# A decoder layer over 16 batches: q and k projected two batches ahead, layer-norm closings moved into the next batch's score stage

## The reference, cut to what matters

```python
# x (16, 256, 128), context (16, 64, 128); all float32
xn  = layernorm(x) * gamma
q, k, v = xn @ w_q, *split(xn @ w_kv)        # 16 heads of 64
q, k = l2norm(q) * q_scale, l2norm(k) * k_scale
s   = 8 * q @ k.T  - slope[head] * distance, with 2 null keys, causal
x   = layernorm(x + softmax(s) @ v @ w_out)
x   = layernorm(x + cross_attention(x, context))   # 16 heads of 8
x   = layernorm(x + ((x @ W1[g].T + b1[g]) @ W2[g].T + b2[g]))  # group g of 2 batches
```

## Time and profile before

| | us |
|---|---|
| median of 3 runs (1008.38 to 1009.17) | 1009.04 |
| the profiled execution's own time | 1014.34 |
| its span, first to last instruction | 1012.2 |
| TensorE busy, of the span | 849.9 (84%) |
| VectorE busy | 802.7 (79%) |
| ScalarE busy | 660.7 (65%) |
| GpSimd busy | 425.7 (42%) |

### The profile page before, as it was taken

The page is one execution under the profiler, slowest core; times in us unless marked ns, Lnnn a source line. Parts: engine busy times, 40 slices in busy tenths (PEclk is TensorE's granted clock), DMA queues, the critical chain, the costliest instruction groups (busy, mean ns, idle before and its releaser), DMA issues.

```text
span 1012.2 us, 18717 instructions
## 1 busy us (share of the span) xinstructions
PE 849.9 (84%) x6181; PEld 663.4 (66%) x6181; DVE 802.7 (79%) x2564; ACT 660.7 (65%) x1938; POOL 425.7 (42%) x356
## 2 busy tenths in 40 slices
PE   6898888888888898888889889888888888888774
PEld 5667666765766676576767657666765766676552
DVE  6665779788888978898897888788787988888545
ACT  4475767757685766767676675767667576766532
POOL 0244162543616253361635346173534617253431
PEclk9799999999999999999999999999999999999795
DMA  6000000000100000000100001000100001000000
GB/s 189 6 1 6 6 27 7 6 12 6 28 12 6 6 13 26 6 6 12 27 6 7 11 6 28 11 6 7 27 11 7 6 12 27 1 6 6 6 1 10
DMA packets 26414, 15.56 MB, mean 15 GB/s; under 512 B 4304, under 2 KB 25552, under 8 KB 26320
## 3 DMA queue, kind: packets, MB, share of 16 engines
q1 hardware_dynamic: 26320, 14.38, 5.0%
HBM read 12.27 MB, written 2.10 MB: 14 GB/s over the span
## 4 chain that ended last, share of the span: by engine, by line
PE 45%; DVE 25%; ACT 18%; issue 6%; POOL 4%; DMA 2%; DVEq 0%; ACTq 0%; POOLq 0%
PE psY L600 12%; ACT pr L1319 9%; PE psS L566 6%; PE psT L586 5%; PE psS L636 4%; ACT sq L1291 3%; POOL pr L1519 3%; PE psJ L441 3%; PE psS L548 3%; PE psJ L443 2%; PE psJ L442 2%; DVE xp L1061 2%; DVE xmax L1059 2%; DVE ssq L957 2%; ACT xpT L1367 2%
## 5 line engine op out<-in xcount | busy, mean ns | idle before, releaser
L1519 POOL TENSOR_TENSOR pr<-pr,rden 128x512 f32<-128x512 f32 x192 | 192.9, 1040 | 379.2 <-ACT pr L1319 195.8
L600 PE MATMUL psY<-val,pT 128*128 128x128 f32 x1536 | 206.5, 281 | 31.3 <-ACT pT L1334 23.7
L1319 ACT ACTIVATE pr<-pr,nmin 128x256 f32<-128x256 f32 (+1 forms) x512 | 225.3, 443 | 10.8 <-DVE nmin L1004 10.2
L600 PEld LDWEIGHTS psY<-val,pT 128*128 128x128 f32 x1536 | 186.6, 193 | 41.8 <-issue 22.2
L1004 DVE CUSTOM_DVE_ANT_0 pr<-psS,alibi,nullmin 128x256 f32<-128x256 f32 (+1 forms) x512 | 183.7, 414 | 26.4 <-PE psS L566 24.4
L1510 POOL TENSOR_TENSOR qk<-qk,rn 128x1024 f32<-128x1024 f32 x64 | 121.1, 1913 | 88.8 <-DVE x L870 50.2
L586 PE MATMUL psT<-ident,pr 128*128 128x128 f32 x768 | 116.9, 279 | 20.2 <-POOL pr L1519 20.2
L566 PE MATMUL psS<-kT,qT 64*128 64x256 f32 (+1 forms) x1024 | 111.7, 346 | 19.3 <-DVE nmin L1004 12.9
L586 PEld LDWEIGHTS psT<-ident,pr 128*128 128x128 f32 x768 | 88.9, 143 | 39.9 <-POOL pr L1519 32.7
L566 PEld LDWEIGHTS psS<-kT,qT 64*128 64x128 f32 x1024 | 78.2, 189 | 48.5 <-DVE nmin L1004 19.4
L1319 ACT ACTIVATION_READ_ACCUMULATOR pr<-pr,nmin 128x1 f32 x512 | 96.6, 189 | 0.0
(11 more groups left out here) (138 smaller groups left out, 1663.5 us busy)
## 6 DMA issues: line engine op xcount, KB each, us to landing
w1s<-w1b SPq DMA_DIRECT2D x8, 258.0 KB, 2.9
xin<-x SPq DMA_DIRECT2D x16, 128.0 KB, 2.1
xres<-x SPq DMA_DIRECT2D x16, 128.0 KB, 2.1
w2s<-w2T SPq DMA_DIRECT2D x8, 256.0 KB, 3.2
out<-x SPq DMA_DIRECT2D x16, 128.0 KB, 1.8
pr<-w_q SPq DMA_DIRECT2D x1, 512.0 KB, 3.8
pr<-w_kv SPq DMA_DIRECT2D x1, 512.0 KB, 5.0
pr<-wvT SPq DMA_DIRECT2D x1, 512.0 KB, 4.5
```

Of the source, the lines that this page charges most:

```text
L600: mm = pe.matmul(psY[t], pT[c % 4][:, P * j:P * (j + 1)], val[:, kt, P * h:P * (h + 1)], start=(blk == 0), stop=False)
L1319: act.activation(pr[t][:, h, :], pr[t][:, h, :], ACT.Exp, bias=nmin[:, t, h:h + 1], scale=-1.0, accum_out=dparts[:, t, h, 0:1]).then_inc(e ...
L1519: pool.tensor_tensor(pr[t][:, hs, :], pr[t][:, hs, :], rden[:, t, hs].unsqueeze(2).broadcast_to([P, heads, P * (t + 1)]), ALU.mult).then_i ...
```

## The change

- q and k are projected for batch `i+2` in iteration `i`, all eight products in stage two, with two buffers of `xnT` and `qk`; all eight copies are ScalarE's. The input is loaded and normed one batch earlier too (`i+3`).
- All eight `project_v(i)` are in iteration `i` itself, in stage one and up to `cross_scores(i-1, 1)`. One copy of the eight stays on VectorE.
- `turn_qk(i+1)` is spread over stage two. The square sums of tile 1 and its `norms(i+1, 1)` are in stage one of the next iteration, as is the whole `norm_qk` on GpSimd for both tiles, ahead of `norm_probs`.
- `x1_turn(i-1)` and `cross_q(i-1)`, `add_y2(i-2)` with `ln3`, `x2_turn`, `feed_forward` and `add_h2(i-2)` with `ln4`'s opening are in stage one; `ln4_end(i-2)` now stands behind `denominators(i, 1)`.
- The score products wait for the copies of q and k that they read, buffers are shared (`xoT` with `x1T`, `xpT` with `pT`, `x2b` with `r1`), the feed-forward has the free half of bank psY, and a few waits guard the shared buffers.
- Iteration 0 prepares batch 1 in one go; the code before the first iteration no longer makes value products.

The diff, cut to its core:

```diff
-QK_DVE, QK_ACT = (0, 1, 3), (2, 4, 5, 6, 7)
+QK_DVE, QK_ACT = (), (0, 1, 2, 3, 4, 5, 6, 7)
...
-            return i + 2 < NB, i + 1 < NB, i >= 1, i >= 2
+            return i + 3 < NB, i + 2 < NB, i + 1 < NB, i >= 1, i >= 2, 1 <= i < NB - 1
...
             def scores(b, t, pair):
-                if t == 0 and pair == 0:
-                    pe.wait_ge(kT_copied, 2 * NT * b + 1)
+                half = pair if t == 0 else pair // 2
+                pe.wait_ge(qT_copied, 2 * NT * b + 2 * t + half + 1)
+                pe.wait_ge(kT_copied, 2 * NT * b + 2 * t + half + 1)
...
             # TensorE, iteration
                 turn_probs(i, 0)
                 turn_probs(i, 1)
+                project_v(i, 4)
                 scores(i, 1, 2)
                 turn_nulls(i, 0)
                 weigh_values(i, 0)
                 turn_probs(i, 2)
+                project_v(i, 5)
                 weigh_values(i, 1)
                 scores(i, 1, 3)
...
                     cross_scores(i - 1, 0)
-                if a:
-                    project_qk(i + 1, 4)
-                    project_qk(i + 1, 5)
-                    project_qk(i + 1, 6)
+                project_v(i, 6)
+                project_v(i, 7)
...
+                if f:
+                    xn_turn(i + 2)
                 if c:
                     cross_scores(i - 1, 1)
...
             # VectorE, iteration
+                if e:
+                    add_y2(i - 2)
+                if p:
+                    sum_squares(i + 1, 1, 0)
                 mask_scores(i, 0, (0, 1))
+                if p:
+                    sum_squares(i + 1, 1, 1)
+                    floor_squares(1)
+                if e:
+                    ln3_begin(i - 2)
                 mask_scores(i, 0, (2, 3))
                 null_shift(i, 0)
+                if e:
+                    ln3_end(i - 2)
+                if p:
+                    norms(i + 1, 1)
...
                 null_shift(i, 1)
-                if c:
-                    cross_shift(i - 1, 0)
                 denominators(i, 1)
+                if e:
+                    ln4_end(i - 2)
                 if c:
+                    cross_shift(i - 1, 0)
                     cross_shift(i - 1, 1)
...
+                if f:
+                    split_xnT(i + 2)
...
             # GpSimd, iteration
+                if c:
+                    x1_plus_bias(i - 1)
+                if p:
+                    norm_qk(i + 1, 0)
+                if e:
+                    x2_plus_bias(i - 2, (i - 2) // 2)
+                if p:
+                    norm_qk(i + 1, 1)
                 norm_probs(i, 0)
+                if c:
+                    spread_values(i)
                 norm_probs(i, 1)
```

More of the change, by code:

```diff
@@ L202, in program @@
         xrden = sb("xrden", [P, NT, XH])
-        xpT = [sb(f"xpT{k}", [P, 512]) for k in range(2)]
+        xpT = pT[0:2]
         r2 = sb("r2", [P, NT, P])
         x2 = sb("x2", [P, NT, P])
-        x2b = sb("x2b", [P, NT, P])
-        x2T = sb("x2T", [P, SEQ])
+        x2b = r1
+        x2T = x1T
         r3 = r2
@@ L622, in cross_q @@
                 pe.wait_ge(x1T_copied, b + 1)
[L623 to L624 removed]
+                take('T1', xqT_copied, b + 1)
+                pe.matmul(psT[1][:, 0:SEQ], xw[:, 0, :], x1T[:], start=True, stop=True).then_inc(xqT_ready, 1)
             def cross_scores(b, t):
@@ L655, in turn_cross_probs @@
                 pe.wait_ge(xprobs_normed, NT * b + t + 1)
-                if k >= 2:
-                    pe.wait_ge(xpT_copied, XC * b + k - 1)
+                take(f'T{half}', xpT_copied, XC * b + k + 1)
                 for j in range(4):
@@ L803, in iteration @@
-                for k in range(4):
-                    if a:
-                        turn_qk(i + 1, 2 * k)
-                        turn_qk(i + 1, 2 * k + 1)
-                    if a and k < 3:
-                        project_v(i + 1, 3 + k)
-                    if a and c and k == 2:
-                        x2_turn(i - 1)
-                    if a and c and k == 3:
-                        feed_forward(i - 1, g)
+                if f:
+                    project_qk(i + 2, 5)
+                if a:
+                    turn_qk(i + 1, 4)
+                    turn_qk(i + 1, 5)
@@ L814, in _ @@
+                if f:
+                    project_nulls(i + 2)
             schedule(iteration)
             b = NB - 1
+            x1_turn(b)
+            cross_q(b)
             for t in range(NT):
@@ L1160, in iteration @@
                 null_shift(i, 1)
+                denominators(i, 1)
+                if e:
+                    ln4_end(i - 2)
                 if c:
                     cross_shift(i - 1, 0)
-                denominators(i, 1)
-                if c:
                     cross_shift(i - 1, 1)
+                if i == 0:
+                    sum_squares(1, 0, 0)
+                    sum_squares(1, 0, 1)
+                    floor_squares(0)
+                    sum_squares(1, 1, 0)
+                    norms(1, 0)
+                    sum_squares(1, 1, 1)
+                    floor_squares(1)
+                    norms(1, 1)
+                if f:
+                    split_xnT(i + 2)
                 if c:
@@ L1416, in iteration @@
                 exponentials(i, 1, (4, 5))
+                copy_v(i, 5)
+                if e:
+                    ln_seed("ln4", (0, 1), i - 1)
                 copy_pT(i, 3)
```

444 lines of the change are left out of this document (229 added, 215 removed).

## The result

The changed kernel takes 1090.7 us (median of 4 runs, 1089.4 to 1091.7), the kernel before 1009.1 beside it (1008.4 to 1009.8). The ratio is 1.0808, with a 95% interval of 1.0789 to 1.0827: 8% slower. The forecast was 1067.0 with a range up to 1083, so the direction was right and the size too small by 24 us.

The account below looks back on a forecast made before the run. Waits between TensorE (84% busy) and VectorE (79%) bound the kernel, with a chain gating stage one. A batch of 35.1 + 26.8 + 1.7 = 63.6 us gave +62 over batches 2 to 13, edges -4: 1009 + 58 = 1067, range 1008 to 1083.

Parts of the forecast that it names:

- Steps 1 to 3: Stage one: tile 1's masks from +8.7 to +11.2, GpSimd's first divisions from 11.6 to 14.9, third score pair 14.2 to 18.3.
- Steps 4 and 5: Late stage one: last mask moves from +20.7 to +25.6, GpSimd's eight divisions of tile 1 from 24.8 to 27.8.
- Step 6: `ln4`'s closing on VectorE beside GpSimd's eight divisions: four dependent steps each wait, 4.5 us instead of 1.1.
- the upper bound of 5.5: `ln4`'s closing takes 5.5 us if its second 128x128 operation waits for GpSimd too.
- rival A: `ln4`'s closing waits once instead of four times: batch 59.5, 1018 us, or 1038 with the clock falling; chance 0.2.
- Step 7: VectorE's two shifts behind the closing, before the second half of `cross_scores`: stage one 35.1 us instead of 26.3.
- Steps 8 and 9: Stage two: TensorE's work falls from 27.68 to 26.8 us with no waits removed; its lower clock behind idling adds 1.7.
- The edges: Start and end: batch 1's start -3, batch 1 -2, batch 14 -2, last batch and tail +3; together -4 us.
- net -3 at the start of batch 1: Six value products leave the time before batch 0, but batch 0 has batch 1's q and k in one line: -3.
- Rival C: Stage two keeps waits, ScalarE's squares standing ahead of copies: 2 us a batch, +24, 1091 us; chance 0.1.
- rival B: Stage one absorbs the moved work: 30.0 + 26.8 = 56.8 us a batch, -23, 986 us; chance 0.14.

Follow-up runs that it names:

- e2: The changed kernel with GpSimd dividing tile 0's probabilities (`norm_probs`) ahead of the next batch's `norm_qk` of tile 1: 1087.0 us, ratio 1.0773 to the kernel before.
- e1: The changed kernel with `ln4_end(i - 2)` ahead of `denominators(i, 1)`, so before GpSimd's eight divisions: 1008.8 us, ratio 0.9994 to the kernel before.
- e12: The changed kernel with the closing of `ln4` behind the first two shifts of `cross_scores` instead of ahead: 1084.7 us, ratio 1.0737 to the kernel before.
- e3: The changed kernel with 36 unused identity transposes on TensorE just ahead of the second half of `cross_scores`: 1067.4 us, ratio 1.0581 to the kernel before.
- e10: e9 with `ln1_end(2)` in batch 0 moved from ahead of tile 1's masks to behind the sixth: 996.7 us, ratio 0.9860 to the kernel before.
- e11: e10 with squares and norms of batch 1's tile 1 behind batch 0's own copies on ScalarE and VectorE: 991.4 us, ratio 0.9816 to the kernel before.
- e6: e1 with last-batch copies of x1 and queries ahead of `ln3`'s seed, and the feed-forward's add ahead of the second denominators: 1004.9 us, ratio 0.9960.
- e4: The changed kernel with batch 0's context projection ahead of batch 1's query/key work, plus e6's reordering of the last batch: 1089.9 us, ratio 1.0803.
- e5: e1 with batch 0 reordered: batch 2's layer norm half behind the masks, its `xn` turn and the context ahead of batch 1's query/key work: 1013.5 us.
- e9: e1 with the edits of e6 and e2 together: 1000.9 us (9 runs, 993.3 to 1006.8), ratio 0.9903 to the kernel before.

## Why the prediction was right and wrong

Against the profiled execution, on which the sum was made, the span grew by 77.6 us (1012.2 to 1089.8), not by 58.

- **Steps 1 to 3** (masks, GpSimd's queue, third score pair): forecast +11.2, +14.9 and +18.3 from the batch's first score product; in the trace +10.8 (438.33), +14.6 (442.17) and +18.0 (445.56). Right, though the 1.6 us that L1036 takes longer beside `norm_qk` were left out; they cost nothing at this place, since the mask of the third pair starts 1.28 us behind it (446.84), as before (415.13). That GpSimd's queue position is what carries the third pair holds as well (e2: +16.7), but it doesn't carry the stage: with the divisions earlier, VectorE's copies were late, and the closing kept its stall.
- **Steps 4 and 5** (last mask, eight divisions): forecast +25.6 and +27.8; +25.5 and +27.6. Right.
- **Step 6** (closing of `ln4`): forecast 4.5 us instead of 1.1, measured 4.1. Right, and the point on which the direction hung: e1 turns 82 us of loss into none by it. Four waits were forecast and four came, but not the same four, and that is luck: the first operation went free, and the second 128x128 operation, which only the upper bound of 5.5 had waiting, did wait (the pair takes 2.02 us and ends with the fourth division). Each waiting operation ends with a GpSimd instruction, and in the changed kernel and in e12 the next division was ahead of the next waiting operation each time, so rival A's single wait did not occur. The Trainium skill (SBUF — State Buffer, Who interferes with whom) speaks of a lock that the first comer keeps for its whole instruction; with the lock these traces agree (0.89 and 0.96 us instead of 0.16, each to the end of a division), and who comes first after it is what only they tell.
- **Step 7** (stage one): forecast 35.1, measured 34.5. **Steps 8 and 9** (stage two and clock): 26.8 + 1.7 = 28.5, measured 28.63, without waits. By e3 the clock's part is 2.05 in this batch. A batch of 63.6 was forecast and 63.13 came; batches 2 to 13 gave +61.8 together where +62 stood. That this is so near is partly luck: batch 6 itself grew by 4.74 us, not 5.2, and the batches with a merged feed-forward, which were not walked through, by more (batch 7 by 6.5).
- **The edges** are the step that failed: "Together -4, bounds -15 and +8". Measured are 77.6 - 61.8 = +15.8, beyond the bound. Their parts: the start of batch 1, forecast -3, came at +11.6; batch 1, -2, at -3.3; batch 14, -2, at -0.9; the last batch and the tail, +3, at +8.4. The first is most of it, and "net -3 at the start of batch 1" is the term that was mis-sized; the prediction shows no working for it. By TensorE's products alone it has the wrong sign: six leave the time before batch 0 (4.7 us at 0.78 each), but batch 0 makes 24 products where it made 16 (6.2 us). Nor did the six come out of the time: batch 0 starts only 1.15 us earlier, behind a wait of 3.43 us for batch 1's normed input.
- **What batch 0 was made of.** It lasts 75.52 us instead of 62.75. Of these 12.8 us TensorE is busy for 8.4 (61.60 instead of 53.23 us, at a granted clock of 0.89 instead of 0.92) and waits for 4.4 (13.9 instead of 9.5). Two of the waits, 4.36 and 4.20 us, come from in-order queues: in VectorE's, a layer norm's second half waits for its seed with the masks behind it; in ScalarE's, the whole preparation of batch 1 stands ahead of the context's keys and of batch 0's own copies. e10 and e11 move just these and shorten batch 0 to 67.47 us. What is left above 62.75 goes with the added work (TensorE is busy 59.05 us in it); no run took that apart. At the end e6 shows 3.9 us of such waits.
- The remaining 4 us of the miss are no mechanism: the profiled execution of the kernel before lay 5.3 above its median, that of the changed kernel 0.9. So 1067.0 + 19.8 - 0.2 + 4.4 = 1091.0, against the measured 1090.7.

Rival C (1091) gives nearly the measured time by a reason that did not occur: stage two has no waits. Of the idea behind rival B, relief of stage two, e1 shows that it is real once the closing is out of the way, though smaller: its batch 6 is 30.5 + 26.55 = 57.0 where B had 30.0 + 26.8 = 56.8, but batches 2 to 13 gain 0.8 us each, where B had 1.6. The batch breaks even at a stage one of 31.6 (58.4 - 26.8); the 31.9 in B counts the edges in.

What stays open: which part of the change brings those 0.8 us, since no run moves q and k alone; what `ln4`'s opening costs beside `norm_qk` in the later kernels, since no run moves it (last section); and how much of the 1.7 us by which the last batch proper grew (997.52 to 1050.31) is anything but its own closing and clock.

## What to carry to other kernels

A short chain of dependent VectorE operations cost about one GpSimd instruction per link where it ran beside a row of GpSimd instructions (here 4.1 and 4.4 us instead of 1.2); look for the gap in which GpSimd idles, and if VectorE waits there anyway the chain is free. When a pipeline is deepened, the sum for the steady batch says nothing of the first one: follow each in-order queue through batch 0 line by line, because the preparation that is spread over a batch elsewhere stands there in one piece, and moving a piece of it past a wait may only hand the wait on (e4, e5). A wait on TensorE can have two prices, its length and the slower matmuls behind it; the second counts only where TensorE's own work is what comes next on the path (2.05 us in e3's batch, nothing in the first pair of the last section).

## What the runs showed of the hardware that I had not expected

Filling TensorE's idle time with matmuls whose result nobody reads made the kernel faster: 36 of them a batch (4.09 us), 23 us in all (e3).

The lower of TensorE's two levels (1.2 of 2.4 GHz) does not follow from the length of the last wait. In e9 the same products start in one batch behind 1.03 us at the higher level, in another behind 1.04 us at the lower:

```profile
353.53 1.14 PE L567 MATMUL psS<-kT,qT 64*128 64x256 f32 x8 [1.03 <-DVE nmin L1019]
...
467.60 1.99 PE L567 MATMUL psS<-kT,qT 64*128 64x256 f32 x8 [1.04 <-DVE nmin L1019]
```

It cost nothing there: both batches last 56.72 us, at granted clocks of 1.00 and 0.97, because the next two waits, 1.19 and 0.90 us in the first, are 0.34 each in the second.

Other batches of the same execution do differ in length. Both of these have a merged feed-forward:

```profile
346.07:402.79 56.72, 50.85 (x383) 40.30 (x382) 45.80 (x155) 41.46 (x125) 26.47 (x22) 1.00 0.06 17
690.29:750.83 60.54, 53.70 (x384) 42.81 (x383) 47.04 (x155) 41.63 (x125) 26.46 (x22) 0.94 0.06 16
```

What parts them begins with VectorE beside GpSimd again. The last operation of `ln4`'s opening takes 0.47 us in the first; in the second it runs beside `norm_qk` (from 707.30) and takes 1.77. The copy behind it is late, and TensorE waits 1.93 us and then takes 1.95 us for products that took 1.13 in the first:

```profile
362.69 0.47 DVE L867 TENSOR_SCALAR ln_small<-ln_mv 128x2 f32<-128x2 f32 x1
...
707.46 1.77 DVE L867 TENSOR_SCALAR ln_small<-ln_mv 128x2 f32<-128x2 f32 x1
...
709.97 1.95 PE L605 MATMUL psY<-val,pT 128*128 128x128 f32 x8 [1.93 <-DVE pT L1045]
```

In batches 2 to 14 of this trace TensorE waits nine times for that copy, each time behind such an operation of 1.03 to 1.86 us; in the four batches where it took 0.47 or 0.48 there is no such wait. So the step on which the direction hung is still there, in small, in this kernel. It would fit that e9's nine runs spread over 13.5 us (993.3 to 1006.8) where the four of the changed kernel spread over 2.3; no run was made to show that.
